# One link of the selection in each of the eight uses, half of the transposes two uses earlier, projection ahead of two late ranks

## The chip, the cores and the metric

The kernel runs on one core of a Trainium2 chip. The metric is the device time of one execution in microseconds (us); of several executions the median is given. The core has five engines that run side by side and meet through semaphores: TensorE (PE in the rows, with its weight loads as PEld), VectorE (DVE), ScalarE (ACT), GpSimd (POOL) and SyncE (SP), whose queue here issues nearly all DMAs. "Q" behind a name (SPq) is the engine's own instruction queue.

## The reference, cut to what matters

```python
def _L0_gnn_ref(A, X, W, b):
    B, N, C, OUT, S = (4, 1024, 128, 128, 25)
    mask = A != 0
    pri = -jnp.arange(N, dtype=jnp.float32)
    scores = jnp.where(mask, pri, neg_inf)
    vals, idx = jax.lax.top_k(scores, S)          # the first 25 neighbours of each node
    valid = vals > neg_inf
    feats = jax.vmap(lambda x, i: x[i])(X, idx)
    feats = jnp.where(valid[..., None], feats, neg_inf)
    agg = feats.max(axis=2)
    degree = mask.sum(axis=-1)
    agg = jnp.where((degree <= S)[..., None], jnp.maximum(agg, 0.0), agg)
    h = jnp.concatenate([X, agg], axis=-1)
    return jax.nn.relu(jnp.einsum('bnf,fo->bno', h, W) + b)

h = jnp.maximum(_layernorm(x, axis=-1), 0.0)      # x: (8, 1024, 128)
return x + _L0_gnn_ref(adj, h, L0_gnn_W, L0_gnn_b)
```

Each of the 8 x 1024 nodes takes the elementwise maximum of the features `h` of its first 25 neighbours, and this and its own features are multiplied by the weights.

## The kernel before, in words

The 8192 rows are worked on in 16 groups of 512, two to a batch. One group is one step of a loop; steps 0, 2, 4, ... are called even here (`u % PER_BATCH == 0`, the first group of a batch), the others odd. The adjacency is turned to a 0/1 mask, transposed by DMA into `mask_t` (8 blocks of 128 neighbours by 512 rows).

**The selection** (`place` on PE, `choose` on ACT) keeps the first 25 neighbours of a row. It is a chain of eight links over the blocks, all in one PSUM bank `side`. Link k on PE is the matmul of L612 (with `rest_w` on block k-1, absent for k = 0) and that of L613 (with `select_w` on block k); ACT then reads `side` and writes `chosen` (L491). L612 of link k+1 waits for L491 of link k, since it overwrites the bank that L491 reads. SP stores `chosen` (L298), block by block, and loads it again in another order as `picks` (L313).

**Ranks** (`ranks` and `late_ranks` on PE, `stage` on ACT) number the chosen neighbours. They go through two PSUM banks in turn (`ring`): matmul k waits until ACT has read matmul k-2 (L483).

**Uses.** The gather of features is done by one-hot matmuls. A use is one `pick_pair` on PE: four matmuls (L655, L656) into one of two double banks `picked`; DVE then takes the maximum into `best` (`take_pair`, L849). A bank is written again by the use after the next one, when DVE has read it. A group has 12 uses. Uses 0 to 3 stand at the end of the step before, uses 4 to 11 at the head of the group's own step. What else PE does is hung behind the picks of a use by tables of numbers: `LATE_WITH` (late ranks 6 and 7 at use 4), `COUNT_WITH` (the count matmuls L636 into the bank `final` at uses 5 and 6), `RANK_WITH` (the ranks of group g+1, uses 5 to 10) and `SELECT_WITH` (the links of group g+2). Before the change the links stand at uses 6, 6, 7, 8, 9, 9, 10, 11, behind the ranks of the same use, on PE and on ACT alike.

**Late rounds.** Neighbours of higher rank are handled in a loop whose count depends on the data. Behind use 7 DVE reduces the count (L841), GpSimd folds it over ten tiny operations (`fold_count`, L426 to L444) and raises `rounds_known`; PE and DVE then load the numbers of rounds from SBUF (L761, L762) and start the loops (`late_round`, `take_late`, L855; `make_late_hot`, L861).

**Around it.** In even steps, behind use 11, `turn_h` transposes the normalized features on PE (L650): four transposes into `side`, when the last link has been read, and four into `final`, when DVE has read the count; ACT copies both to `h_t` (L507). In odd steps GpSimd normalizes the next batch. At the step's end, behind the late rounds, PE does uses 0 to 3 of the next group with late ranks 0 to 5 between them, and then `project` (L680, L682, L686) into `final`, from which DVE makes the result (L868). ACT makes `late` (L496) behind the last link, then the masks of a later group, and SP skews `late` by DMA (L259, L261) and then transposes the masks (L283); `place` of link 0 waits for these transposes (`mask_turned`). The last two steps have no selection left to do.

## Time and profile before

| | us |
|---|---|
| median of 3 runs (lowest, highest) | 716.46 (715.88, 717.83) |
| the profiled execution, its own time | 720.16 |
| its span, first to last instruction | 718.0 |
| PE busy | 600.0 (84%) |
| DVE busy | 570.6 (79%) |
| ACT busy | 405.6 (56%) |
| GpSimd busy | 126.8 (18%) |
| mean granted TensorE clock | 0.989 of full speed |

Busy shares are means over stages with different limits, so the rows below are taken from single steps. In a row of the timeline the first number is the start in us from the span's start, the second how long the instruction or the merged run of instructions (xN) took, then engine, line and operation, output and inputs; in brackets stands how long the engine sat idle before it and what released it. Matmul ends are modelled: two matmuls of 512 columns in a row begin 0.22 us apart though each row says 0.38.

### The profile page before, as it was taken

The numbers are of one execution on the slowest core, as the hardware profiler recorded it, in microseconds if no ns is written. First come the engines' busy times: TensorE is split into PE (matmuls) and PEld (weight loads), VectorE is DVE, ScalarE is ACT, GpSimd is POOL, SyncE is SP. The second block draws the span as 40 slices with busy tenths as digits, with TensorE's granted clock in tenths as the row PEclk, the third lists the DMA queues.
The fourth block names the chain that finished last, engine by engine and source line by source line (L and its number), as shares of the span: only waits on it lengthen the run. The fifth ranks groups of instructions, "written<-read, shape, count | busy, mean of one in ns | idle before, by whom it ended". The sixth has DMA issues, their size and how long they took to land.

```text
span 718.0 us, 10553 instructions
## 1 busy us (share of the span) xinstructions
PE 600.0 (84%) x2928; PEld 264.1 (37%) x2928; DVE 570.6 (79%) x779; ACT 405.6 (56%) x552; POOL 126.8 (18%) x206
## 2 busy tenths in 40 slices
PE   4677897979989898988989889797988889798976
PEld 2222342433434353333433334243433334243333
DVE  4854787879787897878879788787978788788976
ACT  3345747573666836567375654757467674746200
POOL 1301024010420106010150102401051102402020
PEclk9999999999999999999999999999999999999997
DMA  8746856866375735855267660677556352332000
GB/s 330 227 132 212 289 121 216 202 215 176 122 241 109 256 92 197 221 190 181 44 200 216 197 190 15 225 194 229 156 174 213 110 172 50 110 126 74 1 15 16
DMA packets 117486, 115.81 MB, mean 161 GB/s; under 512 B 66003, under 2 KB 102102, under 8 KB 114902
## 3 DMA queue, kind: packets, MB, share of 16 engines
q1 hardware_dynamic: 116310, 114.46, 52.1%
q10 hardware_dynamic: 1152, 1.05, 0.5%
q8 instruction: 12, 0.20, 0.1%
q14 instruction: 12, 0.10, 0.0%
HBM read 58.85 MB, written 20.97 MB: 111 GB/s over the span
## 4 chain that ended last, share of the span: by engine, by line
PE 60%; issue 15%; ACT 11%; DVE 10%; DMA 2%; DVEq 0%; SPq 0%; ACTq 0%
PE picked L655 20%; PE picked L656 18%; PE ring L584 7%; ACT chosen L491 6%; DVE late_hot L861 5%; PE side L612 4%; DVE best L849 3%; ACT late_rank L483 3%; PE side L613 3%; PE final L682 2%; PE final L686 2%; PE final L636 1%; ACT best L514 1%; DMA adj_in<-in_adj_dram 1%; DVE mask L804 1%
## 5 line engine op out<-in xcount | busy, mean ns | idle before, releaser
L849 DVE TENSOR_TENSOR best<-picked,best 128x1024 f32<-128x1024 f32 x160 | 194.3, 1219 | 64.5 <-PE picked L656 64.3
L655 PE MATMUL picked<-late_hot,hi_skew 128*128 128x512 f16 (+1 forms) x536 | 180.8, 350 | 43.6 <-DVE late_hot L861 20.5
L855 DVE TENSOR_TENSOR best<-picked,best 128x1024 f32<-128x1024 f32 (+1 forms) x134 | 141.4, 1055 | 51.1 <-PE picked L656 48.7
L656 PE MATMUL picked<-late_hot,lo_skew 128*128 128x512 f16 (+1 forms) x536 | 180.3, 349 | 0.0
L655 PE MATMUL picked<-hot,h_hi 128*128 128x512 f16 x384 | 147.3, 384 | 5.1 <-DVE best L849 2.8
L656 PE MATMUL picked<-hot,h_lo 128*128 128x512 f16 x384 | 147.1, 383 | 0.0
L514 ACT COPY best<-picked 128x1024 f32<-128x1024 f32 x32 | 31.6, 1013 | 138.6 <-PE picked L656 138.6
L483 ACT ACTIVATE late_rank<-ring,late_bias 128x512 bf16<-128x512 f32 x128 | 81.3, 687 | 46.8 <-PE ring L584 45.0
L861 DVE TENSOR_SCALAR late_hot<-late_rank,numbers 128x2048 f16<-128x2048 bf16 (+1 forms) x166 | 104.0, 627 | 0.0
L491 ACT ACTIVATE chosen<-side,bias_cut 128x512 bf16<-128x512 f32 x120 | 82.2, 685 | 37.9 <-PE side L613 36.2
L483 ACT ACTIVATE rank<-ring,late_bias 128x512 bf16<-128x512 f32 x120 | 79.4, 687 | 37.4 <-PE ring L584 37.4
L655 PEld LDWEIGHTS picked<-late_hot,hi_skew 128*128 128x128 f16 x536 | 52.5, 98 | 124.5 <-issue 60.1
L426 POOL TENSOR_SCALAR late_other<-late_most 1x2 f32<-1x2 f32 x64 | 19.0, 297 | 320.7 <-DVE late_most L841 316.9
L612 PE MATMUL side<-mask_t,rest_w 128*128 128x512 bf16 x105 | 41.9, 399 | 36.9 <-ACT chosen L491 36.0
L656 PEld LDWEIGHTS picked<-late_hot,lo_skew 128*128 128x128 f16 x536 | 52.8, 98 | 37.5 <-issue 2.2
L496 ACT ACTIVATE late<-rank,bias_late 128x1024 bf16<-128x1024 bf16 x60 | 63.8, 1137 | 0.0
L836 DVE TENSOR_SCALAR hot<-rank 128x4096 f16<-128x4096 bf16 x48 | 58.4, 1219 | 0.0
L655 PEld LDWEIGHTS picked<-hot,h_hi 128*128 128x128 f16 x384 | 37.9, 99 | 55.2 <-issue 6.6
L398 POOL TENSOR_TENSOR h<-x_in,moments 128x1024 f32<-128x1024 f32 x8 | 15.7, 1960 | 234.1 <-DVE gain L832 234.1
L656 PEld LDWEIGHTS picked<-hot,h_lo 128*128 128x128 f16 x384 | 37.9, 99 | 40.0 <-issue 1.7
L478 ACT ACTIVATE mask<-adj_in 128x1024 bf16<-128x1024 uint32 x52 | 50.6, 1048 | 0.0
L613 PE MATMUL side<-mask_t,select_w 128*128 128x512 bf16 x120 | 47.5, 396 | 0.5 <-ACT mask_t L523 0.5
(92 smaller groups left out, 529.5 us busy)
## 6 DMA issues: line engine op xcount, KB each, us to landing
adj_in<-in_adj_dram SPq DMA_DIRECT2D x15, 2048.0 KB, 9.0
picks<-kept SPq DMA_DIRECT2D x15, 1024.0 KB, 5.1
kept<-chosen SPq DMA_DIRECT2D x112, 128.0 KB, 3.0
late_skew<-late SPq DMA_DIRECT2D x32, 192.0 KB, 3.6
x_in<-in_x_dram SPq DMA_DIRECT2D x8, 512.0 KB, 6.3
late_skew<-late SPq DMA_DIRECT2D x16, 256.0 KB, 4.8
late_skew<-late SPq DMA_DIRECT2D x32, 128.0 KB, 3.5
xres<-in_x_dram SPq DMA_DIRECT2D x16, 256.0 KB, 2.9
```

The lines of the kernel that those rows point to most:

```text
L478: nc.scalar.activation(mask[:, q, :], counts, ACT.Sign).then_inc(mask_made, 1)
L483: nc.scalar.activation(dst[:, k, :], ring[k % 2][:, :], ACT.Relu, bias=bias).then_inc(ring_read, 1)
L491: nc.scalar.activation((second_chosen if second else chosen)[:, k, :], side[:, :], ACT.Sign, bias=bias_cut[:, 0:1], scale=-1.0).then_inc(c ...
L496: nc.scalar.activation(late[:, 2 * p:2 * p + 2, :], rank[:, s, 2 * p:2 * p + 2, :], ACT.Sign, bias=bias_late[:, 0:1]).then_inc(late_made, 1)
L612: nc.tensor.matmul(side[:, :], rest_w[:, :], turned[:, k - 1, :], start=False, stop=True, skip_group_check=True)
L613: nc.tensor.matmul(side[:, :], select_w[:, :], turned[:, k, :], start=(k == 0), stop=True, skip_group_check=True).then_inc(place_written, 1)
L655: nc.tensor.matmul(dst, hi[:, slot, k, :], onehot, start=start, stop=False)
L656: return nc.tensor.matmul(dst, lo[:, slot, k, :], onehot, start=False, stop=stop)
L836: nc.vector.tensor_scalar(hot[:, (t - 1) % 3, :, :], rank[:, s, :, :], float(t), None, ALU.is_equal).then_inc(hot_made, 1)
L849: nc.vector.tensor_tensor(best[:, half, s, :, :], picked[s][:, :, :], best[:, half, s, :, :], ALU.max).then_inc(picked_read, 1)
L855: nc.vector.tensor_tensor(best[:, s, i, :, 0:width], picked[i][:, :, 0:width], best[:, s, i, :, 0:width], ALU.max).then_inc(late_read[i], 1)
L861: nc.vector.tensor_scalar(late_hot[:, part, 0:width], late_rank[:, part, 0:width], which, None, ALU.is_equal).then_inc(late_hot_made[i], 1)
```

## The change

Three edits of order, none of an operation. First, `SELECT_WITH` spreads the eight links over uses 4 to 11, one in each, and within a use the link stands ahead of the ranks, on PE and on ACT. Second, `turn_h` is split: in even steps the four transposes into `final` stand at use 9, those into `side` stay at use 11, and the bank `final` now takes features 0 to 3 and `side` 4 to 7; ACT copies both behind use 11 as before. Third, at the step's end `project` stands ahead of late ranks 4 and 5.

```diff
--- before.py
+++ after.py
@@ -54,9 +54,9 @@
     def spread_over(first, last):
         return [[k for k in range(K) if use == first + k * (last - first + 1) // K] for use in range(USES)]
 
-    SELECT_WITH, RANK_WITH = spread_over(6, 11), spread_over(5, 10)
+    SELECT_WITH, RANK_WITH = spread_over(4, 11), spread_over(5, 10)
     LATE_EARLY, LATE_WITH, COUNT_WITH, COUNT_USE, LATE_HOT_USES = 6, {4: (6, 7)}, (5, 6), 7, (8, 9)
-    LATE_USES, HIGH_USE, TURN_USE = {11: (0, 1, 2, 3)}, 8, 11
+    LATE_USES, HIGH_USE, TURN_USES = {11: (0, 1, 2, 3)}, 8, (9, 11)
     STATS_USES, MOMENTS_USE = (7, 8), 9
 
     CHAINS, LINK = 4, 2
@@ -500,12 +500,12 @@
                 act.wait_ge(moments_made, K * batch + K)
                 nc.scalar.activation(spread[:, :], moments[:, :, 1], ACT.Sqrt, bias=bias_eps[:, 0:1]).then_inc(spread_made, 1)
 
-            def turned_h(batch, slot):
+            def turned_h(batch, slot, n):
                 dst = h_t[:, slot, :, :, :].rearrange("c h q (a n j) -> c n j (h q) a", n=2, j=4)
-                for n, bank in enumerate((side, final)):
-                    act.wait_ge(h_written, 2 * batch + n + 1)
-                    nc.scalar.copy(dst[:, n, :, :, :],
-                                   bank[:, :].rearrange("c (j b a) -> c j b a", j=4, b=PER_BATCH * Q)).then_inc(h_turned, 1)
+                bank = (final, side)[n]
+                act.wait_ge(h_written, 2 * batch + n + 1)
+                nc.scalar.copy(dst[:, n, :, :, :],
+                               bank[:, :].rearrange("c (j b a) -> c j b a", j=4, b=PER_BATCH * Q)).then_inc(h_turned, 1)
 
             def first_maxima(g, s, half):
 
@@ -549,14 +549,15 @@
                 for use in range(PAIRS, USES):
                     for k in LATE_WITH.get(use, ()):
                         stage(at + REST_AT, k, late_rank, late_bias[:, k:k + 1])
+                    for k in SELECT_WITH[use] if not at_end(it, u, 2) else []:
+                        choose(g + 2, k)
                     for k in RANK_WITH[use] if more else []:
                         stage(at + RANK_AT, k, rank[:, (u + 1) % 2], late_bias[:, 0:1])
-                    for k in SELECT_WITH[use] if not at_end(it, u, 2) else []:
-                        choose(g + 2, k)
                     for p in LATE_USES.get(use, ()) if more else []:
                         find_late(p, (u + 1) % 2, at + RANK_AT + 2 * p + 2)
-                    if use == TURN_USE and u % PER_BATCH == 0:
-                        turned_h(batch_of(it, u), (u // PER_BATCH) % 2)
+                    if use == TURN_USES[1] and u % PER_BATCH == 0:
+                        for n in range(2):
+                            turned_h(batch_of(it, u), (u // PER_BATCH) % 2, n)
                 if not at_end(it, u, 3):
                     make_masks((u + 1) % 2, range(Q))
                 if u % PER_BATCH == 0 and not at_end(it, u, PER_BATCH):
@@ -638,17 +639,17 @@
                 if i == LINK - 1:
                     last.then_inc(count_written, 1)
 
-            def turn_h(batch, chosen, counted):
+            def turn_h(batch, n, chosen, counted):
 
                 pe.wait_ge(normed_made, batch + 1)
-                for n, bank in enumerate((side, final)):
-                    if n == 0:
-                        pe.wait_ge(chosen_made, chosen)
-                    else:
-                        pe.wait_ge(late_reduced, counted)
-                    for j in range(4):
-                        last = nc.tensor.transpose(bank[:, j * P:(j + 1) * P], h32[:, 4 * n + j, :], eye32[:, :])
-                    last.then_inc(h_written, 1)
+                if n == 0:
+                    pe.wait_ge(late_reduced, counted)
+                else:
+                    pe.wait_ge(chosen_made, chosen)
+                bank = (final, side)[n]
+                for j in range(4):
+                    last = nc.tensor.transpose(bank[:, j * P:(j + 1) * P], h32[:, 4 * n + j, :], eye32[:, :])
+                last.then_inc(h_written, 1)
 
             def pick(dst, hi, lo, k, onehot, slot, start, stop):
 
@@ -748,12 +749,12 @@
                         late_ranks(g, at + REST_AT, k)
                     if use in COUNT_WITH:
                         count(g, COUNT_WITH.index(use))
+                    for k in SELECT_WITH[use] if not at_end(it, u, 2) else []:
+                        place(g + 2, k)
                     for k in RANK_WITH[use] if more else []:
                         ranks(g + 1, at + RANK_AT, k)
-                    for k in SELECT_WITH[use] if not at_end(it, u, 2) else []:
-                        place(g + 2, k)
-                    if use == TURN_USE and u % PER_BATCH == 0:
-                        turn_h(batch_of(it, u), K * GROUPS if at_end(it, u, 2) else K * (g + 3), g + 1)
+                    if use in TURN_USES and u % PER_BATCH == 0:
+                        turn_h(batch_of(it, u), TURN_USES.index(use), K * GROUPS if at_end(it, u, 2) else K * (g + 3), g + 1)
 
                 pe.reg_add(known_due, known_due, 2)
                 pe.wait_ge(rounds_known, 2)
@@ -781,11 +782,13 @@
                 if more:
                     for k in (0, 1):
                         late_ranks(g + 1, at + LATE_AT, k)
-                    for use in (2, 3):
-                        pick_pair(g + 1, use, next_slot)
-                        for k in (2 * use - 2, 2 * use - 1):
-                            late_ranks(g + 1, at + LATE_AT, k)
+                    pick_pair(g + 1, 2, next_slot)
+                    for k in (2, 3):
+                        late_ranks(g + 1, at + LATE_AT, k)
+                    pick_pair(g + 1, 3, next_slot)
                 project(g, it, u)
+                for k in (4, 5) if more else ():
+                    late_ranks(g + 1, at + LATE_AT, k)
 
             over_groups(pe, step)
 
```

The order that this gives in an even step. PE, from the end of use 5 to use 7, before (L636 is the count, L584 with `picks` a rank, L613 and L612 the links; other rows are register and wait instructions):

```order
L656 MATMUL picked<-hot,h_lo 128x512
L636 MATMUL final<-late_skew,half_ones 32x512 x4
L579 REGISTER_ALU
L584 MATMUL ring<-picks,half_w 128x512
L603 REGISTER_ALU
L613 MATMUL side<-mask_t,select_w 128x512
L611 ISA
L612 MATMUL side<-mask_t,rest_w 128x512
L613 MATMUL side<-mask_t,select_w 128x512
L667 REGISTER_ALU
```

PE, from use 4's late ranks to use 5's link, with the change (lines are one higher):

```order
L585 MATMUL ring<-late_skew,half_ones 128x512
L604 ISA
L614 MATMUL side<-mask_t,select_w 128x512
L668 REGISTER_ALU
L656 MATMUL picked<-hot,h_hi 128x512
L657 MATMUL picked<-hot,h_lo 128x512
L656 MATMUL picked<-hot,h_hi 128x512
L657 MATMUL picked<-hot,h_lo 128x512
L637 MATMUL final<-late_skew,half_ones 32x512 x4
L612 ISA
L613 MATMUL side<-mask_t,rest_w 128x512
L614 MATMUL side<-mask_t,select_w 128x512
```

Link 0 stood behind use 6's rank, with link 1 right behind it; now link 0 stands at use 4, and the picks and the count of use 5 stand between it and link 1.

ACT, the head of the same step, before:

```order
L483 ACTIVATE rank<-ring,late_bias 128x512
L482 REGISTER_ALU
L483 ACTIVATE rank<-ring,late_bias 128x512
L489 ISA
L490 ISA
L491 ACTIVATE chosen<-side,bias_cut 128x512
L490 REGISTER_ALU
L491 ACTIVATE chosen<-side,bias_cut 128x512
```

and with the change:

```order
L483 ACTIVATE late_rank<-ring,late_bias 128x512
L489 ISA
L490 ISA
L491 ACTIVATE chosen<-side,bias_cut 128x512
L490 REGISTER_ALU
L491 ACTIVATE chosen<-side,bias_cut 128x512
L482 REGISTER_ALU
L483 ACTIVATE rank<-ring,late_bias 128x512
L482 REGISTER_ALU
L483 ACTIVATE rank<-ring,late_bias 128x512
```

The first `chosen` stood behind three ranks; now it follows the two late ranks, and the second stands ahead of the ranks of its use.

PE, the end of use 11 before:

```order
L612 MATMUL side<-mask_t,rest_w 128x512
L613 MATMUL side<-mask_t,select_w 128x512
L646 ISA
L650 MATMUL side<-eye,h 128x128 x4
L650 MATMUL final<-eye,h 128x128 x4
L758 REGISTER_ALU
```

PE, the end of use 9 with the change (L651 is the transposes' line there):

```order
L613 MATMUL side<-mask_t,rest_w 128x512
L614 MATMUL side<-mask_t,select_w 128x512
L580 REGISTER_ALU
L585 MATMUL ring<-picks,half_w 128x512
L644 ISA
L651 MATMUL final<-eye,h 128x128 x4
```

and the end of use 11:

```order
L612 REGISTER_ALU
L613 MATMUL side<-mask_t,rest_w 128x512
L614 MATMUL side<-mask_t,select_w 128x512
L648 ISA
L651 MATMUL side<-eye,h 128x128 x4
L759 REGISTER_ALU
```

The transposes into `final` moved from behind those into `side` to behind use 9's rank.

## Rows read from the trace of the kernel before

**Rows 1.** Waits: engine, line waited for, total us, times, longest us.
```profile
PE side L612 <- ACT chosen L491: 36.0, 49, 1.1
```

**Rows 2.** Timeline of PE in step 6 (even), use 4 to the late rounds.
```profile
310.17 0.38 PE L655 MATMUL picked<-hot,h_hi 128*128 128x512 f16 x1
...
314.93 0.38 PE L613 MATMUL side<-mask_t,select_w 128*128 128x512 bf16 x1
316.45 0.39 PE L612 MATMUL side<-mask_t,rest_w 128*128 128x512 bf16 x1 [1.14 <-ACT chosen L491]
316.67 0.38 PE L613 MATMUL side<-mask_t,select_w 128*128 128x512 bf16 x1
...
321.58 0.39 PE L612 MATMUL side<-mask_t,rest_w 128*128 128x512 bf16 x1 [0.21 <-ACT chosen L491]
...
322.97 0.39 PE L612 MATMUL side<-mask_t,rest_w 128*128 128x512 bf16 x1 [0.78 <-ACT chosen L491]
...
327.39 0.66 PE L650 MATMUL side<-eye,h 128*128 128x128 f32 x4 [0.78 <-ACT chosen L491]
...
329.33 0.39 PE L655 MATMUL picked<-late_hot,hi_skew 128*128 128x512 f16 x1 [0.84 <-issue]
```

**Rows 3.** Timeline of PE in step 7 (odd), the same stretch.
```profile
355.98 0.38 PE L655 MATMUL picked<-hot,h_hi 128*128 128x512 f16 x1
...
371.81 0.39 PE L612 MATMUL side<-mask_t,rest_w 128*128 128x512 bf16 x1
...
373.75 0.39 PE L655 MATMUL picked<-late_hot,hi_skew 128*128 128x512 f16 x1 [1.33 <-DVE best L849]
```

**Rows 4.** Timeline of ACT in step 6.
```profile
311.45 1.27 ACT L483 ACTIVATE late_rank<-ring,late_bias 128x512 bf16<-128x512 f32 x2 [2.54 <-PE ring L584]
...
315.71 0.68 ACT L491 ACTIVATE chosen<-side,bias_cut 128x512 bf16<-128x512 f32 x1
317.09 0.69 ACT L491 ACTIVATE chosen<-side,bias_cut 128x512 bf16<-128x512 f32 x1 [0.70 <-PE side L613]
```

**Rows 5.** Timeline of DVE in step 6, uses 7 to 11.
```profile
317.95 1.23 DVE L849 TENSOR_TENSOR best<-picked,best 128x1024 f32<-128x1024 f32 x1 [2.25 <-PE picked L656]
319.10 0.68 DVE L841 TENSOR_REDUCE late_most<-final 128x2 f32<-128x512 f32 x1
...
323.04 1.21 DVE L849 TENSOR_TENSOR best<-picked,best 128x1024 f32<-128x1024 f32 x1
...
325.38 2.32 DVE L849 TENSOR_TENSOR best<-picked,best 128x1024 f32<-128x1024 f32 x2
```

**Rows 6.** Timeline of DVE in step 7: the count's reduction, the takes of uses 10 and 11.
```profile
364.90 0.68 DVE L841 TENSOR_REDUCE late_most<-final 128x2 f32<-128x512 f32 x1
...
370.28 1.23 DVE L849 TENSOR_TENSOR best<-picked,best 128x1024 f32<-128x1024 f32 x1 [0.51 <-PE picked L656]
371.79 1.22 DVE L849 TENSOR_TENSOR best<-picked,best 128x1024 f32<-128x1024 f32 x1 [0.28 <-PE picked L656]
```

**Rows 7.** Timeline of GpSimd: the fold's last operation in steps 6, 7 and 14.
```profile
323.79 0.20 POOL L444 TENSOR_SCALAR late_rounds<-late_full 1x1 int32<-1x1 f32 x1 [0.16 <-POOL late_full L440]
...
370.33 0.20 POOL L444 TENSOR_SCALAR late_rounds<-late_full 1x1 int32<-1x1 f32 x1 [0.16 <-POOL late_full L440]
...
654.99 0.20 POOL L444 TENSOR_SCALAR late_rounds<-late_full 1x1 int32<-1x1 f32 x1 [0.16 <-POOL late_full L440]
```

**Rows 8.** Timeline of PE in step 14 (no selection): the first late round.
```profile
657.08 0.39 PE L655 MATMUL picked<-late_hot,hi_skew 128*128 128x512 f16 x1 [1.71 <-DVE best L849]
```

**Rows 9.** The line of the mask transposes in step 3 (odd): starts, time to landing.
```profile
L283 SPq DMA_TRANSPOSE mask_t<-mask x4: 1278/1452/2370, 212.4 to 216.7; - x4
...
DMA to landing us min/median/max: 3.9/4.4/5.2
```

**Rows 10.** Timeline of PE: late ranks 6 and 7 behind use 4, step 4.
```profile
223.95 0.59 PE L584 MATMUL ring<-late_skew,half_w 128*128 128x512 bf16 x2
```

**Rows 11.** Timeline of DVE at the head of step 6: the take of use 4.
```profile
311.23 1.23 DVE L849 TENSOR_TENSOR best<-picked,best 128x1024 f32<-128x1024 f32 x1 [0.17 <-PE picked L656]
```

## The prediction, made before the changed kernel had run

> **What bounds the kernel now.** I read the page's engine shares first: PE is busy 84%, DVE 79%, and neither is full, so the places where PE waits decide. The view of waits names the largest one in the region that the change touches: L612 behind L491, 36.0 us in 49 times [rows 1], that is, a link of the selection that waits for ACT to have read the one before. The timeline shows the pattern of a step, and it repeats to the hundredth in all 14 steps that have a selection. A matmul of 512 columns takes 0.22 us of PE's row (316.45 to 316.67). In step 6 link 0 starts at 314.93, so PE is free at 315.15, but link 1 starts at 316.45: 1.30 us stand. L612 then waits again at 321.58 and 322.97, and the transposes at 327.39, with 0.21, 0.78 and 0.78 us in brackets [rows 2]. Brackets count from the modelled end; against the pitch of 0.22 these are 0.37, 0.94 and 0.94, and use 11's link, without a bracket, stands another 0.22.
>
> Why links wait: ACT starts `chosen` 0.42 us after L613 starts (316.67 to 317.09), and L612 starts 0.74 us after `chosen` (315.71 to 316.45) [rows 2, 4]. So from L613 to the next L612 there must lie 1.16 us. Two links at one use have 0.22 between them; the first, besides, finds ACT busy with a rank (its `chosen` starts at 315.71, 0.78 after L613 and not 0.42).
>
> **PE's account of an even step.** From the first pick of use 4 (310.17) to the first transpose (327.39) are 17.22 us [rows 2]. Waits of the selection are 1.30 + 0.37 + 0.94 + 0.22 + 0.94 = 3.77; what is left, 13.45, is work: 32 picks, 3 late-rank matmuls, 8 ranks and 15 link matmuls at 0.216 are 12.5, and the two counts with small gaps the rest (0.43 each). In the odd step 7 the same account runs from 355.98 to the last link at 371.81 [rows 3]: 15.83 us, of which 2.83 are waits.
>
> **The change, first edit, even steps.** I replay the order with these durations from 310.17. Nothing ahead of it moves (third edit, below).
> - Use 4: picks and late ranks end at 311.68, link 0 takes until 311.90. ACT has the two late ranks from 311.45 [rows 4], 0.58 each, so `chosen` 0 starts at 312.62 and link 1 may start at 313.36. PE, with the picks and the count of use 5 behind it, is there at 313.19. New wait: 0.17.
> - Uses 5 to 8: a use is picks 0.86, link 0.43, and one or two ranks of 0.22, so from L613 to the next L612 lie 0.22 + 0.22 + 0.86 = 1.30 or more, over the 1.16 needed. ACT has one `chosen` and one or two ranks in that time, 1.16 or 1.74 against PE's 1.51 or 1.73: it keeps up, and since `chosen` now stands first, a late rank delays no link. The ring asks that rank k-2 be read; the closest is rank 6 at 320.7, and ACT has read rank 4 by 320.5.
> - DVE becomes the limit of use 11. Use 7's last pick starts at 316.80 and its take at 317.22, where before it was 317.95. From there DVE has takes, count, statistics and one-hots back to back: takes 9 and 10 start 5.09 and 7.43 us behind take 7 [rows 5], hence at 322.31 and 324.65. Use 11 needs take 9 done, 1.3 us after its start: 323.6. PE, with the first half of the transposes (0.49) now behind use 9, would be there at 322.84. New wait: 0.72 to 0.76.
> - The second half of the transposes still waits for the last link: 0.95.
> In all PE does 13.45 + 0.49 and waits 0.17 + 0.74 + 0.95, which puts the transposes into `side` at 325.97; adding the steps of the replay one by one gives 325.80. I take 325.85. Before, the late rounds started 1.94 us after the first transpose (327.39 to 329.33). I take this as the time from the last wait's release to the end of the loads of the round numbers, since step 7 has the same 1.94 after its last link (371.81 to 373.75) although two matmuls follow there and eight transposes here [rows 2, 3]. Late rounds: 327.79, a gain of 1.54.
>
> **Odd steps.** Without statistics and transposes PE reaches its last L612 at 371.81 - 2.83 + 0.17 for link 1 and 0.2 for DVE at use 11: 369.35, plus 1.94 is 371.3. But the loads also wait for GpSimd's fold. It ends at 370.53, 5.63 us after the reduction starts (364.90) [rows 6, 7]. The reduction follows take 7, which comes 0.73 earlier, no more. So the fold ends at 369.80. Step 14, where nothing of the selection stands, shows what follows a fold that is last: 655.19 to 657.08, 1.89 us [rows 7, 8]. Late rounds: 369.80 + 1.88 = 371.68 where they were 373.75, a gain of 2.07. In even steps the fold ends at 323.99 and has room.
>
> On the fold the Trainium skill has a rule. The fold takes 4.89 us in step 6 (319.10 to 323.99) and 5.63 in step 7 [rows 5 to 7], with the same operations. GPSIMD Engine Reference, section Specifications, says that GpSimd shares its SBUF interfaces with VectorE and meets contention with DVE instructions in a two-port mode or with two SBUF inputs; step 7 has a cast of DVE in the fold's time that step 6 lacks, and this fits. By that rule the length is set by what DVE does meanwhile; DVE's sequence behind the reduction stays, so I keep 5.63. With 4.89 the gain would be 2.4 (PE's own 371.3).
>
> **Second edit** moves 0.49 us of transposes from the end into use 9; since the start of the late rounds counts from the wait's release, it brings nothing at the end, and at use 9 it is hidden by the wait for DVE at use 11. Its wait for the reduction (319.1) is long over. Net: 0, bounded by 0 to 0.49 gained in seven steps.
>
> **Third edit**: `project` comes 0.65 us (three matmuls) earlier, the late ranks 2.3 later. DVE's result is earlier, but its next take waits for use 4's picks (311.23, 0.17 idle [rows 11]), which end when they did. ACT reads ranks 4 and 5 from 309.94 and is free for rank 6 at 311.45 as before. Net: 0, bounded by 0.2 us a step either way.
>
> **What is moved past SP.** Link 0 waits for the mask transposes, and it comes 3.2 us earlier in the step (311.68 against 314.93). The narrowest case is behind a short odd step: the last of the four issues at 216.7 and lands 3.9 to 5.2 us later, by 221.9 [rows 9]; link 0 would stand behind the late ranks of 223.95, at 224.6 [rows 10]. 2.7 us are left, and both sides move by about the same 2 us. `late` (L496) follows the last `chosen` and comes 1.5 to 2.5 us earlier, so its skew does too.
>
> **Sum.** Seven even steps by 1.54 and seven odd by 2.07: 10.8 + 14.5 = 25.3 us. Steps 14 and 15 have no links: 0. Span 718.0 - 25.3 = 692.7, the profiled execution's own time 720.16 - 25.3 = 694.9. The median is 0.995 of that execution, so 691 us.
>
> **Rivals.**
> - *The start hangs on take 11.* In step 7 the late rounds start 0.74 us after use 11's take ends (371.79 + 1.22 = 373.01 to 373.75) [rows 3, 6], and the profile names it as releaser. The code asks at that point only for take 10, but the numbers fit. In the odd step take 7 comes 0.73 earlier, and the idle before takes 10 and 11 (0.51 and 0.28 in brackets, some 0.16 more each by the pitch of takes [rows 6]) closes for the most part: take 11 some 1.7 earlier, gain 1.7; even steps as above. 7 x 1.54 + 7 x 1.7 = 22.7: 694 us.
> - *The loads run ahead.* Then even steps start when the array is done (326.4 + a short gap) and gain 2.0 to 2.8, odd ones stay on the fold: 14 + 14.5 = 28.5 or more, 688 us. Against it speaks the 0.84 us of "issue" behind the transposes though the fold was done at 323.99 [rows 2, 7]. The Trainium skill speaks for it: Advanced Engine Details and Errata, section Sequencer and Instruction Queues, has engine instructions wait in a queue while the sequencer already starts control instructions. In this trace the loads show no such lead.
> - *ACT falls behind.* Its 1.74 us in uses with two ranks leaves nothing against PE's 1.73. If links and ring reads there cost PE a further ACT operation (0.58) at two uses, a step gives back 1.16: 25.3 - 16.2 = 9.1 us gained, 707 us.
> - *Link 0 waits for the masks: slower.* If in the seven odd steps the transposes landed x us later relative to use 4, because skew, stores and loads crowd SP's queue and the DMA engines earlier, PE would stand x - 2.7 there. From x = 6.3 the gain of 25.3 is gone; at 8, 7 x 5.3 = 37, slower by 12: 728 us. The measured spread of landings is 1.3 us, which speaks against it.
> - *No change*: the waits come back whole, as PE meets DVE at every use. DVE's own work from take 7 on is in the replay already; it would have to be 1.8 us a step longer. 716 us.
>
> **How the numbers follow.** Forecast 0.50, take 11 0.16, run ahead 0.12, ACT behind 0.14, no change 0.04, masks 0.04. The likeliest is 691. The unknown costs (third edit 0.2 a step, second up to 3.4 in all, a link's latency) make 687 to 696 of it; down to 685 and up to 702 takes in both neighbours and part of the ACT case. Faster by over 0.3% (2.1 us, about what a measurement can tell from no change): 0.92; within 0.3% 0.04; slower 0.04.
>
> **What would show it.** Right: L612's wait for L491 falls from 36.0 us to about 7 (6 ahead of the loop, and at most 0.1 a step); link 1's bracket is 0.17 or less in place of 1.14; a wait of PE for L849 (one line higher now) of 0.5 to 0.7 at use 11 of even steps; the late rounds of step 6 start 17.6 us behind the first pick of use 4 (19.16 before), those of step 7 15.7 (17.77 before), with the fold ending 1.9 us ahead. Wrong: brackets at the links of uses 6 to 10, which would be ACT; a wait of link 0 for a DMA; or late rounds longer than before, which would mean that DVE's one-hots or its own loads are now last.

## The result, and the profile after

The changed kernel took 696.65 us (median of 4 runs, 696.43 to 698.24) where the kernel before took 716.49 beside it: a ratio of 0.9725, 95% interval [0.9706, 0.9745], 19.8 us less. The forecast was 691, most likely 687 to 696 and at the widest 685 to 702. The profiled execution took 696.69, span 694.6; the one before 720.16 and 718.0.

The page of the changed kernel, part 1 and the rows of slices (tenths of 40 slices; PEclk is the granted clock):

```profile
PE 596.5 (86%) x2928; PEld 265.9 (38%) x2928; DVE 573.6 (83%) x779; ACT 401.3 (58%) x552; POOL 126.7 (18%) x206
...
PEclk9879999999999999999999999999999999999998
```

Its mean granted clock is 0.974 of full speed, where it was 0.989. That mean takes in the start of the program: in this profile the 13 us from 30 to 43 ran at 0.50. So the clock is read below from single stretches, and not from the mean.

The waits of PE in the changed kernel (L613 is the link's first matmul there; total us, times, longest):

```profile
PE side L613 <- ACT chosen L491: 6.2, 7, 1.1
...
PE side L651 <- ACT chosen L491: 5.5, 7, 0.9
```

The links' 36.0 us [rows 1] are down to 6.2, all of it in the first 57 us, ahead of the loop: no step's link waits for ACT any more. The transposes' wait stays. Step 6 on PE, the rows that answer to [rows 2]:

```profile
299.31 0.38 PE L656 MATMUL picked<-hot,h_hi 128*128 128x512 f16 x1
...
302.49 0.39 PE L613 MATMUL side<-mask_t,rest_w 128*128 128x512 bf16 x1
...
312.73 0.39 PE L656 MATMUL picked<-hot,h_hi 128*128 128x512 f16 x1 [0.55 <-DVE best L852]
...
314.98 0.66 PE L651 MATMUL side<-eye,h 128*128 128x128 f32 x4 [0.78 <-ACT chosen L491]
...
316.91 0.61 PE L656 MATMUL picked<-late_hot,hi_skew 128*128 128x512 f16 x1 [1.27 <-DVE best L852]
317.31 0.63 PE L657 MATMUL picked<-late_hot,lo_skew 128*128 128x512 f16 x1
```

Counted from the first pick of use 4, link 1 comes after 3.18 us (3.19 in the replay), use 11's picks after 13.42 (13.4), the transposes after 15.67 (15.63 to 15.8), the late rounds after 17.60 (17.62; 19.16 before). Step 7, answering to [rows 3], [rows 6] and [rows 7], on PE:

```profile
345.11 0.38 PE L656 MATMUL picked<-hot,h_hi 128*128 128x512 f16 x1
...
360.76 0.39 PE L656 MATMUL picked<-late_hot,hi_skew 128*128 128x512 f16 x1 [1.72 <-DVE best L852]
```

The same step of the changed kernel on DVE:

```profile
353.31 0.68 DVE L844 TENSOR_REDUCE late_most<-final 128x2 f32<-128x512 f32 x1
...
359.23 1.21 DVE L852 TENSOR_TENSOR best<-picked,best 128x1024 f32<-128x1024 f32 x1
```

And on GpSimd, the end of the fold:

```profile
358.74 0.20 POOL L444 TENSOR_SCALAR late_rounds<-late_full 1x1 int32<-1x1 f32 x1 [0.16 <-POOL late_full L440]
```

15.65 us from use 4 to the late rounds (15.70 forecast, 17.77 before); the fold takes 5.63 us as before and ends 1.82 us ahead of the rounds. Use 11's take ends at 360.44, only 0.32 us ahead, where it was 0.74: the start does not hang on it.

What the forecast did not have is in the last two rows of step 6. The late matmuls are 0.40 and then 0.43 us apart, not 0.22. DVE's first take stood 1.93 us behind the first late matmul before (331.26, bracket 2.43) and now waits longer:

```profile
320.40 1.23 DVE L858 TENSOR_TENSOR best<-picked,best 128x1024 f32<-128x1024 f32 x1 [3.13 <-PE picked L657]
```

The granted clock in that stretch, from the view by windows (the clock is the number behind the engines' busy times, third from the end):

```profile
316.90:319.90 3.00, 2.99 (x8) 1.07 (x9) 0.36 (x1) 3.00 (x5) 0.00 (x0) 0.50 0.72 221
319.90:322.90 3.00, 2.67 (x13) 1.06 (x12) 2.50 (x3) 3.00 (x5) 0.00 (x0) 0.97 0.90 366
```

The same view of the kernel before, at the head of its step 6, and of the changed kernel at the head of step 8:

```profile
329.33:332.33 3.00, 3.00 (x14) 1.37 (x15) 1.07 (x1) 3.00 (x5) 0.00 (x0) 1.00 0.68 229
...
401.05:404.05 3.00, 3.00 (x14) 1.39 (x15) 1.42 (x2) 3.00 (x5) 0.00 (x0) 1.00 0.64 227
```

0.50 is the lower of TensorE's two levels, 1.2 GHz and not 2.4; in it eight matmuls begin in 3 us and not fourteen. The take comes 3.49 us behind the first matmul and not 1.93, and the late rounds of this step are 1.55 us longer (19.69 for 18.14). Such a start is called slow below. The changed kernel's profile has one in steps 1, 2, 6, 12 and 15 (0.50 to 0.55 in the first 3 us of each), the profile before in steps 0 and 15 only.

The sum over the two profiles: from use 4 to the late rounds, steps 1 to 13 gained 23.6 us, where the forecast has 23.7 for them. Four slow starts (steps 1, 2, 6 and 12) took back 6.2, and the end gained 0.9, so from use 4 of step 1 on the profiles are 18.2 us apart. Up to there they are 5.2 apart (104.03 and 98.86), more than the 1.54 forecast for step 0. That part can't be put down to the change: the profile before had the lower clock in some of it (0.65 from 61 to 65), and its execution took 3.7 us over its kernel's median, which the changed kernel's did not. This is why the profiles are 23.4 us apart and the medians 19.8.

At the end of step 0 PE waits 2.02 us for the skew of `late` (next row). The kernel before has no such wait in its loop; six of the kernels below have it too, with 0.7 to 2.8 us in all.

```profile
91.20 0.88 PE L585 MATMUL ring<-late_skew,half_w 128*128 128x512 bf16 x2 [2.02 <-DMA late_skew<-late]
```

The masks of step 3 come no later than link 0 needs them [rows 9, 10]: the last of the four issues at 209.4 and lands by 215.1, the link stands at 217.24, 2.1 us left of the 2.7.

```profile
L283 SPq DMA_TRANSPOSE mask_t<-mask x4: 1282/1685/2472, 204.6 to 209.4; - x4
...
DMA to landing us min/median/max: 4.2/4.7/5.7
```

The first matmul of link 0 that reads them, on PE:

```profile
217.24 0.38 PE L614 MATMUL side<-mask_t,select_w 128*128 128x512 bf16 x1
```

### The profile page after: what moved, and what is told of

The parts are those of the page before. It is cut to its first block, busy times and chain, and to the rows that moved or that the text cites. A ratio compares the mean times of both kernels' runs of the same rounds, so it can differ in the third digit from the quotient of the medians.

```text
span 694.6 us, 10561 instructions
## 1 busy us (share of the span) xinstructions
PE 596.5 (86%) x2928; PEld 265.9 (38%) x2928; DVE 573.6 (83%) x779; ACT 401.3 (58%) x552; POOL 126.7 (18%) x206
## 4 chain that ended last, share of the span: by engine, by line
PE 47%; DVE 18%; issue 16%; ACT 7%; DMA 4%; POOL 3%; DVEq 2%; SPq 2%; ACTq 0%; POOLq 0%
PE picked L656 17%; PE picked L657 15%; DVE late_hot L864 6%; PE ring L585 5%; DVE best L852 5%; ACT late_rank L483 3%; PE final L683 2%; PE final L687 2%; PE side L613 2%; ACT chosen L491 2%; DMA kept<-chosen 1%; DVE stats L822 1%; ACT best L514 1%; PE side L614 1%; POOL late_other L426 1%
## 5 line engine op out<-in xcount | busy, mean ns | idle before, releaser
L656 PE MATMUL picked<-late_hot,hi_skew 128*128 128x512 f16 (+1 forms) x536 | 183.8, 356 | 49.0 <-DVE best L852 24.2
L657 PE MATMUL picked<-late_hot,lo_skew 128*128 128x512 f16 (+1 forms) x536 | 183.0, 354 | 0.0
L839 DVE TENSOR_SCALAR hot<-rank 128x4096 f16<-128x4096 bf16 x48 | 62.6, 1305 | 0.0
L585 PE MATMUL ring<-late_skew,half_w 128*128 128x512 bf16 x128 | 42.0, 389 | 9.0 <-ACT late_rank L483 6.2
```

Of the source, the lines that this page charges most:

```text
L585: last = nc.tensor.matmul(ring[k % 2][:, :], w[:, :], m, start=(i == 0), stop=(i == len(terms) - 1))
L656: nc.tensor.matmul(dst, hi[:, slot, k, :], onehot, start=start, stop=False)
L657: return nc.tensor.matmul(dst, lo[:, slot, k, :], onehot, start=False, stop=stop)
L839: nc.vector.tensor_scalar(hot[:, (t - 1) % 3, :, :], rank[:, s, :, :], float(t), None, ALU.is_equal).then_inc(hot_made, 1)
```

## The experiments

Theory: the links' spread is the whole gain, step by step as replayed, and the shortfall of 5.7 us against the forecast is the granted clock at the head of the late rounds. Rivals: the other two edits matter; the order within a use matters; the bound of the even or of the odd steps is another one.

All results, with steps 6 and 7 from the first pick of use 4 to the late rounds, and the steps whose first take came over 2.2 us behind the first late matmul (1.93 otherwise), from one profiled execution each. Beside these kernels the one before had medians of 715.0 to 717.1 (single runs 711.7 to 719.8), so differences of 2 us between two kernels are read from the steps, not from the medians.

| kernel | median us | ratio to before [95%] | step 6 | step 7 | slow first takes, steps |
|---|---|---|---|---|---|
| before | 716.5 | 1 | 19.16 | 17.77 | 0, 15 |
| changed | 696.65 | 0.9725 [0.9706, 0.9745] | 17.60 | 15.65 | 1, 2, 6, 12, 15 |
| links only | 693.74 | 0.9691 [0.9631, 0.9751] | 17.60 | 15.69 | 1, 2, 10, 15 |
| transposes together | 693.63 | 0.9681 [0.9611, 0.9752] | 17.60 | 15.65 | 0, 1, 2, 15 |
| projection late | 697.81 | 0.9746 [0.9684, 0.9808] | 17.60 | 15.69 | 0, 1, 2, 4, 8, 10, 12, 15 |
| links behind ranks | 699.06 | 0.9764 [0.9703, 0.9824] | 17.45 | 15.53 | 0, 1, 2, 6, 10, 12, 14, 15 |
| changed, PE kept busy | 688.25 | 0.9593 [0.9554, 0.9633] | 17.63 | 15.68 | none |
| before, PE kept busy | 715.36 | 0.9987 [0.9963, 1.0011] | 19.20 | 17.82 | none |
| statistics early | 693.09 | 0.9673 [0.9629, 0.9717] | 16.88 | 15.68 | 1, 2, 15 |
| count early | 695.96 | 0.9696 [0.9655, 0.9737] | 17.08 | 16.02 | 1 to 7, 10, 12 |
| kept busy, statistics early | 684.82 | 0.9571 [0.9536, 0.9607] | 16.87 | 15.66 | none |
| the same, links behind ranks | 687.23 | 0.9601 [0.9571, 0.9631] | 17.39 | 15.64 | none |
| count early, subtraction held | 683.61 | 0.9558 [0.9512, 0.9604] | 17.06 | 14.78 | 10, 15; by DVE, not by the clock: 1, 3, 5, 7, 9, 11, 13 |
| all together | 688.68 | 0.9622 [0.9593, 0.9650] | 17.73 | 15.99 | none |

**The first edit alone.** On the kernel before:

```diff
-    SELECT_WITH, RANK_WITH = spread_over(6, 11), spread_over(5, 10)
+    SELECT_WITH, RANK_WITH = spread_over(4, 11), spread_over(5, 10)
...
-                    for k in RANK_WITH[use] if more else []:
-                        ranks(g + 1, at + RANK_AT, k)
                     for k in SELECT_WITH[use] if not at_end(it, u, 2) else []:
                         place(g + 2, k)
+                    for k in RANK_WITH[use] if more else []:
+                        ranks(g + 1, at + RANK_AT, k)
```

(and the same on ACT.)

> The first edit alone on the kernel before (links at uses 4 to 11, ahead of the ranks; all transposes behind use 11, projection behind the late ranks). Theory: the whole gain is the links', and the other two edits are hidden, so 696 to 699 us; in an undisturbed odd step 15.7 us from the first pick of use 4 to the late rounds, in an even one 17.6 to 18.1. Rival: the split transposes and the projection carry a part; then this run lies 3 us or more above the changed kernel (over 700).

693.74 us is 2.3 under the band. One slow start less in the loop (three and not four) is 1.6 of it; the rest is open, and the two intervals overlap. Steps 6 and 7 are those of the changed kernel to 0.04 us. The links are the whole gain.

**The transposes together again, and the projection late again.** On the changed kernel:

```diff
-                    if use in TURN_USES and u % PER_BATCH == 0:
-                        turn_h(batch_of(it, u), TURN_USES.index(use), ...)
+                    if use == TURN_USES[1] and u % PER_BATCH == 0:
+                        for n in range(2):
+                            turn_h(batch_of(it, u), n, ...)
```

> The changed kernel with all eight transposes behind use 11, those into final first, so that they fall into the wait for the last link. Theory: the late rounds start 1.93 us behind the last wait's release in either case, so the same 17.6 us in even steps and 695 to 698 us; and since PE is busy 0.5 us more shortly ahead of the late rounds, TensorE's granted clock may fall in fewer steps (each such step costs 1.54 us), then 691 to 694. Rival: the half at use 9 fills a wait that is otherwise lost, then 0.4 us more in each of 8 even steps, about 700.

```diff
-                project(g, it, u)
-                for k in (4, 5) if more else ():
+                    for k in (4, 5):
                         late_ranks(g + 1, at + LATE_AT, k)
+                project(g, it, u)
```

> The changed kernel with the projection behind late ranks 4 and 5 again. Theory: the projection's place is worth nothing on the path (0 to 0.1 us a step), 695 to 699 us. Rival: the late ranks ahead of use 4 push ACT and the first links; then link 1 waits longer and this run is 0.2 us a step or more away, either way (under 694 or over 700).

Steps 6 and 7 do not move in either (17.60; 15.65 and 15.69): both edits are worth nothing in the order, as forecast. The totals differ by 4 us, and the slow first takes are 4 against 8; whether the place of the transposes or of the projection makes a slow start likelier, one execution of each cannot tell.

**Links behind the ranks.** On the changed kernel, `SELECT_WITH` behind `RANK_WITH` again on PE and ACT.

> The changed kernel with each link behind the ranks of its use again, on PE and ACT. Theory: what counts is one use between two links (1.30 us or more against 1.16 needed); behind two ranks chosen comes 0.3 us later and one link waits under 0.2 us, so 696 to 699 us. Rival: standing ahead of the ranks matters as much as the spread; then ACT's rank (0.58 us) delays each of eight links and 20 to 40 us come back, 705 to 720.

The order within a use is not what counts here: steps 6 and 7 are even 0.15 and 0.12 us shorter, though one link a step waits for ACT again (14 times 0.21 us in brackets, 2.9 in all). The total is 2.4 us higher, with three more slow starts, and the intervals of the two ratios overlap. At this point the clock was the likeliest account of the shortfall, and it was still only argued.

**PE kept busy.** On the changed kernel, and on the kernel before:

```diff
+            def keep_busy(n):
+                for _ in range(n):
+                    nc.tensor.matmul(ring[0][:, :], half_w[:, :], filler[:, :], start=True, stop=True)
...
+                    if use == USES - 1:
+                        pe.wait_ge(ring_read, (at + RANK_AT if more else at + REST_AT) + K - 1)
+                        keep_busy(4)
...
+                if u % PER_BATCH == 0:
+                    keep_busy(4)
                 pe.reg_add(known_due, known_due, 2)
```

> The changed kernel, with PE kept busy where it waits ahead of the late rounds: four idle matmuls of 512 columns (0.86 us, into a ring bank that nobody needs then) behind use 11's link, and in even steps four more behind the transposes. They change no result. Theory (the shortfall is TensorE's granted clock: in 4 to 8 of 16 steps the first late matmuls run at half speed and the round's first take comes 3.5 us behind them and not 1.93): the takes come at 1.93 us in nearly all steps, granted clock over 0.985, starts of the late rounds unchanged (17.6 and 15.7 us behind use 4), 687 to 691 us. Rival: the slow starts are no matter of PE's pauses there; then as many as before, and 696 or more.

> The kernel before with the same idle matmuls. Theory: its profile had a slow first take only in steps 0 and 15, so there is little to win: 0 to 3 us, 712 to 716. Rival: the idle matmuls help by something else than the clock (or the clock costs the kernel before as much); then 5 us or more here too, under 711.

Step 6 on PE in the changed kernel with it (line numbers are higher):

```profile
309.38 0.39 PE L659 MATMUL picked<-hot,h_hi 128*128 128x512 f16 x1 [0.56 <-DVE best L865]
...
310.69 1.03 PE L709 MATMUL ring<-filler,half_w 128*128 128x512 bf16 x4
...
312.12 1.03 PE L709 MATMUL ring<-filler,half_w 128*128 128x512 bf16 x4
...
313.60 0.39 PE L659 MATMUL picked<-late_hot,hi_skew 128*128 128x512 f16 x1 [0.45 <-issue]
```

The view by windows at the head of its late rounds (the clock is again the third number from the end):

```profile
313.60:316.60 3.00, 3.00 (x14) 1.38 (x15) 1.39 (x2) 3.00 (x5) 0.00 (x0) 1.00 0.63 232
```

96 idle matmuls take 24.6 us of PE's busy time and make the kernel 8.4 us faster: 688.25, the interval of its ratio (up to 0.9633) clear of the changed kernel's (from 0.9706). The late rounds of step 6 start where they did (17.63 us after use 4), and no step has a slow take. The two profiles are 7.9 us apart (694.6 and 686.7), and the five slow starts that are gone make up just that: 1.62, 1.54, 1.56, 1.54 and 1.62 us in steps 1, 2, 6, 12 and 15. Other differences, of up to 1.9 us each and mostly ahead of use 4 of step 3, cancel. So what the idle matmuls win back is the clock.

On the kernel before the same matmuls give 0.9987 [0.9963, 1.0011], nothing that can be told from no change. The kernel before has no slow start in steps 1 to 14 in either of its two profiles, with idle matmuls and without; each kernel with the links spread and no idle matmuls has one to nine of them there. So it is the change that brings them, as far as one profiled execution of the kernel before can show it.

The 5.7 us between 691 and 696.65 are of the size of the four slow starts, 6.2 us, but they can't be divided to the end. The wait for the skew adds 2.0, step 0 may have gained more than its 1.54, and the profile of the kernel before lay 3.7 us over its median, so that its start can't be taken as typical.

**DVE's statistics early.** On the changed kernel:

```diff
-    STATS_USES, MOMENTS_USE = (7, 8), 9
+    STATS_USES, MOMENTS_USE = (5, 6), 6
```

> The changed kernel with DVE's statistics of the next batch behind uses 5 and 6 and not 7 and 8, and their aggregation behind use 6 and not 9, where DVE idled. Theory: in even steps use 11 waits 0.7 us for DVE because of these; that wait goes, and the late rounds start 17.0 us behind use 4, not 17.6; odd steps stay at 15.7. 4 us less but for the clock: 690 to 694. Rival: DVE is not what even steps wait for; then 17.6 stays.

The wait ahead of use 11's picks is gone, and the transposes' is not:

```profile
311.19 0.38 PE L656 MATMUL picked<-hot,h_hi 128*128 128x512 f16 x1
...
313.43 0.66 PE L651 MATMUL side<-eye,h 128*128 128x128 f32 x4 [0.78 <-ACT chosen L491]
315.37 0.39 PE L656 MATMUL picked<-late_hot,hi_skew 128*128 128x512 f16 x1 [1.28 <-issue]
```

16.88 for 17.60: DVE is what step 6 waited for, as the replay had it, and 1.94 us from the transposes' release to the late rounds (313.43 to 315.37) holds here too. Of the other even steps 2, 8, 10 and 12 gain 0.7 to 0.9 us, step 4 only 0.1: from its transposes' release to the late rounds are 3.00 us there, and why is open.

**The count early.** On the changed kernel:

```diff
-    LATE_EARLY, LATE_WITH, COUNT_WITH, COUNT_USE, LATE_HOT_USES = 6, {4: (6, 7)}, (5, 6), 7, (8, 9)
+    LATE_EARLY, LATE_WITH, COUNT_WITH, COUNT_USE, LATE_HOT_USES = 6, {4: (6, 7)}, (4, 5), 6, (8, 9)
```

> The changed kernel with the count's matmuls behind uses 4 and 5 and its reduction behind use 6, a use (1.5 to 1.9 us) earlier each. Theory: odd steps wait for GpSimd's fold; with the fold early they start their late rounds when PE's own row lets them, 0.4 us or up to 1.1 earlier than 15.7, so 14.6 to 15.3; even steps stay at 17.6. 3 to 7 us less but for the clock: 689 to 694. Rival: the start hangs on use 11's take; then 15.7 stays (a take does not move).

A miss in both parts. Steps 14 and 15, where the fold is last, start their late rounds 1.5 and 1.4 us earlier, so that bound is real. Even steps gain 0.5, which fits DVE having the reduction off its row earlier. But odd steps are 0.35 us longer. Step 9 of this kernel on DVE:

```profile
444.42 0.75 DVE L864 TENSOR_SCALAR late_hot<-late_rank,numbers 128x2048 f16<-128x2048 bf16 x1
445.10 1.21 DVE L852 TENSOR_TENSOR best<-picked,best 128x1024 f32<-128x1024 f32 x1
446.23 2.68 DVE L864 TENSOR_SCALAR late_hot<-late_rank,numbers 128x2048 f16<-128x2048 bf16 x1
448.83 2.34 DVE L852 TENSOR_TENSOR best<-picked,best 128x1024 f32<-128x1024 f32 x2
```

And on GpSimd (L386 is the subtraction for the low part of the next batch):

```profile
446.24 2.12 POOL L386 TENSOR_TENSOR h_lo<-h,h_hi 128x1024 f16<-128x1024 f32 x1
```

The same one-hot takes 0.75 and then 2.68 us, and the second starts with the subtraction, which follows the fold. Takes 10 and 11 begin 14.58 us after use 4, where in step 9 of the changed kernel they begin after 12.99. The theory that follows, that GpSimd's subtraction holds DVE up, is tested next.

**The subtraction held back.** On the kernel of the last run:

```diff
+                        pool.wait_ge(picked_read, g * READ + 9)
                         low_part(batch_of(it, u + 1), ((u + 1) // PER_BATCH) % 2)
```

> The changed kernel with the count a use earlier, and GpSimd's subtraction for the low part of the next batch (2.1 us, odd steps) held back until DVE has taken use 10. Theory: in the run with the early count alone this subtraction began together with DVE's one-hots of use 9, which then took 2.68 us where it is 0.75, and that, not the fold, set the start of odd steps (16.0 us). Held back, the one-hots take 0.75 and odd steps start their late rounds after 15.0 to 15.3 us. Rival: GpSimd is not the cause of the 2.68; then it and the 16.0 stay.

Step 7 of this kernel on DVE:

```profile
348.99 0.74 DVE L865 TENSOR_SCALAR late_hot<-late_rank,numbers 128x2048 f16<-128x2048 bf16 x1
349.65 2.34 DVE L853 TENSOR_TENSOR best<-picked,best 128x1024 f32<-128x1024 f32 x2
351.91 2.24 DVE L840 TENSOR_SCALAR hot<-rank 128x4096 f16<-128x4096 bf16 x1
```

And on GpSimd:

```profile
350.94 2.13 POOL L386 TENSOR_TENSOR h_lo<-h,h_hi 128x1024 f16<-128x1024 f32 x1 [2.24 <-DVE best L853]
```

The one-hot is back at 0.74, the takes beside the subtraction keep their 2.34 for two, and the next one-hot operation, 1.22 us with no subtraction beside it, takes 2.24. Odd steps start after 14.78 us, 0.2 sooner than the theory had it. This is the fastest kernel of the study, 683.61 us.

The changed kernel has the same overlap, where it costs nothing: the subtraction runs there from 358.91 to 361.03, and this one-hot takes 1.75 us in step 7:

```profile
360.36 1.75 DVE L839 TENSOR_SCALAR hot<-rank 128x4096 f16<-128x4096 bf16 x1
```

In both kernels it ends 1.08 us behind the subtraction's end (362.11; 354.15 against 353.07), nearly its own length; the 2.68 of the smaller one-hot end 0.55 behind (448.91 against 448.36). This reads as if the one-hot stood until GpSimd was done; no run tests that reading by itself. It also explains the first takes of 2.2 to 2.3 us in the odd steps of this kernel: DVE is in the one-hot until 354.15 and begins the take at 354.08. The clock was low at the head of steps 10 and 15 only.

**Combinations.** The edits are those above.

> The changed kernel with the eight idle matmuls and with the statistics behind uses 5 and 6. Theory: both gains stand beside each other: no slow first takes, even steps 16.9 us, odd ones 15.7; 688.3 (idle matmuls alone) less 7 times 0.7 is 683 us, 681 to 685. Rival: with DVE's wait gone the idle matmuls come late and hold PE up at the transposes; then even steps stay at 17.3 or more and the run over 686.

> The same with each link behind the ranks of its use. Theory: with the clock held, the order by which even steps were 0.15 and odd ones 0.1 us shorter shows in the time: 1 to 2 us under the run without it, 680 to 683. Rival: its 5 us more without idle matmuls were the order's own and not the clock's; then 686 or more.

> The changed kernel with all of it: idle matmuls, statistics behind uses 5 and 6, links behind ranks, count a use earlier, subtraction held back. Theory: as the run with idle matmuls, early statistics and links behind ranks, less 0.4 to 0.6 us in seven odd steps and 1.4 in each of the last two: 674 to 679 us. Rival: with the count at use 6 as well DVE is full there, and use 8 or 9 waits for it; then no gain over that run.

The first holds: 684.82, steps 16.87 and 15.66. The second does not: 687.23 lies over 686, on the side of the rival that the order itself costs time. Step 6 is 0.5 us longer (17.39), and 0.37 of it is a link that waits. In the view of waits the links stand at 9.1 us in 21 times, 14 more than the 7 ahead of the loop, just as in the kernel with the links behind the ranks alone; step 6 has this one, at the use behind the two ranks:

```profile
306.14 0.39 PE L616 MATMUL side<-mask_t,rest_w 128*128 128x512 bf16 x1 [0.21 <-ACT chosen L494]
```

Standing ahead of the ranks is worth nothing in even steps while PE waits for DVE at use 11 anyway, and counts as soon as that wait is gone.

All together misses too, with 688.68 for 674 to 679, and is no gain over the second. The links wait 28 times there, 21 of them in the loop. In its step 7 two links wait (0.21 us each in brackets, 0.37 by the pitch of 0.22), and the last link comes 13.97 us after use 4, where it comes after 13.01 in the kernel with the count early and the subtraction held. From there to the late rounds are 2.02 us, with four idle matmuls between, against 1.77. So of the 1.2 us by which this odd step is longer (15.99 for 14.78) 1.0 lies ahead of the last link, and most of it is the order of links and ranks. The fastest kernel with links ahead of the ranks and idle matmuls placed for its own pauses was not tried.

## Why the prediction was right, and where it was not

**What bounds the kernel.** Right. The links' waits were real time on the path, and all of it went: 6.2 us ahead of the loop remain.

**Even steps.** Right in size and in kind: 17.60 us against 17.62, with the two waits that were forecast to remain (DVE at use 11, ACT at the transposes) and no other. The early statistics confirm the first: without it 16.88. The account of PE's work by 0.216 us a matmul and the 1.16 us from link to link carried it. Link 1's forecast wait of 0.17 is a gap of 0.14 ahead of 302.49, without a bracket. Steps 2, 4 and 12 took 0.1 to 0.4 us more than 17.60, as they had taken 0.1 to 0.3 more than 19.16 before. Most of it lies behind the last wait's release: from there to the late rounds are 2.06, 2.35 and 2.10 us in these steps, and 1.93 to 1.94 in steps 6, 8 and 10. The prediction took 1.94 for all; why these three are longer is open.

**Odd steps.** Right: 15.65 against 15.70, with GpSimd's fold in the place that was forecast. The fold kept its 5.63 us in step 7, and 1.82 us lie from its end to the late rounds, where 1.88 were forecast. In all eight odd steps of the changed kernel these are 1.82 to 1.87; before, where PE's last link was later than the fold, they were 2.8 to 3.3 in the seven with links. With the count early and the subtraction held the same step starts after 14.78, which confirms the fold as what it waited for.

**Second and third edit, and what is moved past SP.** Right at nothing: the runs without them have the same steps. The masks had 2.1 us left. The 2.02 us wait for the skew at the end of step 0 was not foreseen: the prediction had the skew only come earlier.

**The sum.** 25.3 us were forecast; of the 23.7 that fall to steps 1 to 13 the order gave 23.6. But the step "so the median is 691" failed by 5.7 us, and the term at fault is one that was missing: the granted clock. It was read as 0.989 in the table of before and held constant. The wait for the skew was missing too. By the total alone the rival with take 11 (694) lay nearer; it is the steps that tell the two apart.

Step 15 of the profile before shows the fall of the clock: PE idles 2.6 us ahead of its late rounds, and six matmuls later they are 0.43 us apart. In the changed kernel PE's pauses in even steps lie behind use 10: 0.55, 0.78 and 1.27 us in brackets within 5 us. Counted by the pitch of the matmuls (an estimate from the rows), PE stood 3.1 of the last 6 us ahead of the late rounds of step 6, against 2.1 before and 1.4 with idle matmuls. The clock is then at 0.50 for the first 3 us of the late rounds, in 4 of the 14 steps with links. Each costs some 1.55 us since DVE's take waits for eight matmuls. With the pauses filled the time is 688.25, 2.8 us under the forecast, so the order is worth somewhat more than was forecast, or step 0 gained more than its 1.54; which of these is open.

The pauses do not decide it alone: steps 6, 8 and 10 have the same ones to 0.02 us, and only step 6 was slow. Step 1 was slow after PE had stood 2.6 of the last 6 us, and in step 7 of the kernel before it stood as long without a fall. What picks the step is open. The Trainium skill's page TensorE: Matmul & The Clock Gate has two sections on this: "HAM oscillation — how this bites in real kernels", where PE falls back to half rate between bursts that wait for DMA, and "A second HAM failure mode: psum-queue depth-cycling", where short idles between groups of matmuls do it (HAM is the page's name for the monitor that gates the clock). The rows above agree with the second: the pauses wait for DVE and ACT, not for DMA, and the clock is 0.50 in the 3 us stretch behind them, 1.00 with the pauses filled.

**The rivals.** Take 11: false, its end is 0.32 us ahead of the rounds in step 7 and 0.74 before, so no fixed time lies between the two. Run ahead: false, even steps gained 1.56 and not 2.0 to 2.8, and the 1.93 to 1.94 us from release to rounds stand in three kernels (327.39 to 329.33, 314.98 to 316.91, 313.43 to 315.37). ACT behind: false in this kernel; with links behind the ranks a shadow of it shows, 0.2 us a wait in brackets. Masks: false, and no change: false.

**The Trainium skill's rule on GpSimd** (GPSIMD Engine Reference, Specifications: the SBUF interfaces are shared with VectorE, with contention against a two-port mode or two SBUF inputs) was used on the fold's length alone, where it changed nothing. Its weight lay on the other side, DVE waiting for GpSimd: 2.68 us for 0.75, found only when the early count missed. The runs agree that the two get in each other's way; in which mode the one-hot runs, none of them shows.

## What to carry to other kernels

A chain between two engines costs nothing once other work of at least the round trip stands between its links; measure the round trip in the trace (here 1.16 us) and lay the tables out by it. A replay of one step from measured durations gave each new wait here to some hundredths, but it holds the clock fixed: where an edit leaves PE's waits bunched ahead of a burst that someone waits for, look at the granted clock there, stretch by stretch, and try idle matmuls in the pause before counting the gain. An edit that brings an engine's work forward also brings forward what is queued behind it.

## What the runs showed of the hardware that was not expected

- Idle matmuls, 24.6 us of PE's busy time, made a kernel 8.4 us faster (688.25 against 696.65), by holding the granted clock: 1.00 at the head of step 6's late rounds, where it was 0.50. The same on the kernel before: a ratio of 0.9987. The mean clock of a whole execution does not show this: that kernel before with idle matmuls had 0.982 and no slow start.
- A one-hot of DVE (128x2048, bf16 to f16) that began with GpSimd's subtraction took 2.68 us where it takes 0.75; one of 128x4096 that began during it took 1.75 and 2.24 for 1.22, ending 1.08 us behind it each time. DVE's takes beside the same subtraction (two in 2.34 us) took no longer than elsewhere.
- From the release of PE's last wait to the first matmul of a loop whose count is loaded from SBUF there were 1.93 to 1.94 us, whether two matmuls (step 7 before), four transposes (step 6 of the changed kernel) or eight (step 6 before) stood between. It is no constant: in step 4 of the changed kernel it was 2.35, with the statistics early 3.00.
